# Two interleaved units of a four-layer decoder on one core: own chains, own attention jobs and tables of turns in the second part

## The reference, cut to what matters

```python
# layer 2
x += linear_attention(norm(x)) @ w_proj          # L2a: elu(q)+1, elu(k)+1, causal, 16 heads
x += latent_cross_attention(norm(x), ctx)        # L2x: 16 heads of 64, keys = context and latents
x  = moe_lora_ffn(norm(x))                       # L2f: router, 8 low-rank experts, the best 2
# layer 3
x += delta_rule_mixer(norm(x), conv3, conv15, conv64, gates)  # L3a: triangular inverse per chunk,
                                                 #   three filters, moments, gelu, softmax over 5 paths, rms
x += rotary_cross_attention(norm(x), ctx)        # L3x
x += moe_ffn(norm(x))                            # L3f: 8 experts, the best 2, and a shared one
```

## Time and profile before

| | |
|---|---|
| median of 3 runs | 1779.44 us |
| the profiled execution, its own time | 1794.3 us |
| its span | 1792.9 us |
| mean granted TensorE clock | 0.871 of full |
| part a, first to last matmul | 480.9 us |
| part c, four iterations | 1161.4 us |

### The profile page before, as it was taken

How to read it: one execution, slowest core, us unless ns; L and a number is a source line. 1 busy time by engine, 2 the same in 40 slices (tenths; PEclk the granted TensorE clock), 3 DMA queues, 4 the chain that set the end, 5 groups by cost and what they waited for, 6 DMA issues and landing times. The chain is left out here.

```text
span 1792.9 us, 40153 instructions
## 1 busy us (share of the span) xinstructions
PE 1530.7 (85%) x17496; PEld 1300.6 (73%) x17496; DVE 1100.9 (61%) x2843; ACT 670.3 (37%) x1323; POOL 127.9 (7%) x265
## 2 busy tenths in 40 slices
PE   5888887898886899898879999779989977989986
PEld 3666676776654589797769788668879766978865
DVE  5668678577768566355658445567644565753565
ACT  4343463453547535222315323323422231532331
POOL 2010111111110000100000100000000000010000
PEclk8699998898997889898779988789988777998878
DMA  6000000000000100000000000000000000000000
GB/s 245 1 2 1 1 2 1 1 2 1 2 30 30 61 1 1 1 4 1 1 1 1 1 3 2 1 1 2 1 2 3 1 1 1 1 1 2 3 1 24
DMA packets 6510, 19.87 MB, mean 11 GB/s; under 512 B 2240, under 2 KB 4288, under 8 KB 5824
## 3 DMA queue, kind: packets, MB, share of 16 engines
q1 hardware_dynamic: 6336, 17.32, 2.7%
HBM read 16.27 MB, written 1.05 MB: 10 GB/s over the span
## 5 line engine op out<-in xcount | busy, mean ns | idle before, releaser
L480 PE MATMUL PS<-CC 128*128 128x256 f32 x656 | 197.1, 449 | 20.4 <-DVE mv L457 16.9
L480 PEld LDWEIGHTS PS<-CC 128*128 128x128 f32 x656 | 142.3, 229 | 45.7 <-DVE mv L457 17.7
L1839 PE MATMUL PS<-AR 64*64 64x32 f32 (+1 forms) x3072 | 124.3, 237 | 16.4 <-DVE AR L2112 8.5
L1839 PEld LDWEIGHTS PS<-AR 64*64 64x64 f32 x3072 | 121.5, 156 | 18.1 <-DVE AR L2112 9.0
L469 POOL TENSOR_SCALAR SC<-mv 128x2 f32<-128x2 f32 x96 | 18.6, 194 | 1568.9 <-DVE mv L457 1567.0
L587 PEld LDWEIGHTS PS<-vo,AR 128*64 128x64 f32 x2560 | 111.8, 178 | 25.1 <-issue 15.9
L587 PE MATMUL PS<-vo,AR 128*64 128x18 f32 x2560 | 121.4, 241 | 5.7 <-DVE AR L1493 3.9
L1855 PE MATMUL PS<-AR,PA 64*64 64x204 f32 (+39 forms) x2624 | 123.3, 323 | 2.8 <-issue 2.1
L567 PE MATMUL PS<-CC,AR 128*128 128x128 f32 x512 | 100.7, 343 | 19.9 <-ACT AR L551 19.9
L1855 PEld LDWEIGHTS PS<-AR,PA 64*64 64x64 f32 x2624 | 104.1, 144 | 10.7 <-issue 4.8
L531 DVE TENSOR_REDUCE SC<-PS 128x8 f32<-128x512 f32 x128 | 86.5, 684 | 21.8 <-PE PS L691 21.1
(11 more groups left out here) (405 smaller groups left out, 3114.3 us busy)
## 6 DMA issues: line engine op xcount, KB each, us to landing
WC<-in_cw SPq DMA_DIRECT2D x1, 5438.5 KB, 19.3
PA<-in_fd SPq DMA_DIRECT2D x1, 2624.0 KB, 9.9
PA<-in_stat SPq DMA_DIRECT2D x2, 1280.0 KB, 5.7
out<-X SPq DMA_DIRECT2D x1, 1024.0 KB, 5.1
PA<-in_aw SPq DMA_DIRECT2D x1, 975.0 KB, 10.8
AR<-in_raw SPq DMA_DIRECT2D x1, 832.0 KB, 7.5
CC<-in_const SPq DMA_DIRECT2D x1, 809.0 KB, 7.6
AR<-in_intw SPq DMA_DIRECT2D x1, 576.0 KB, 8.5
```

The costliest lines, as they stand in the source:

```text
L480: T.matmul(st.ps[:, bank, 0:ST], lhsT=ident, rhs=CC[:, 0:ST], start=True, stop=True)
L1839: m = T.matmul(ps[rows, bank, n * width:(n + 1) * width], lhsT=lhs[rows, n, :], rhs=rhs(rows, n), start=True, stop=True)
```

## The change

All of it is in part c. The cross-attention jobs of L2x become a list for each stream with shorter lags, their stages in another order inside a step and with a yield behind each; the shared chains of L3a and L3f become one chain for each stream, with a yield ahead of each wait; the two table loads and the exponential are issued for each stream; and the four tables `AHEAD_C` get uneven numbers. No matmul is added or taken away, nor is a `keep_clock`.

```diff
-        LAG = {"scores": 1, "turn": 4, "weigh": 5, "out": 6}
-        JOBS = [(st, j) for j in range(TS * GR) for st in streams]
+        LAG = {"scores": 1, "turn": 2, "weigh": 3, "out": 3}
+        JOBS = range(TS * GR)
...
-        def tensor_cross():
+        def tensor_cross(st):
             G2, O2 = (cross_w[:, m:m + 2, :, :].rearrange("p m c d -> p (m c) d") for m in (0, 2))
             for n in range(len(JOBS) + LAG["out"]):
-                for st, j in at_lag(n, 0):
+                for st, j in at_lag(st, n, LAG["weigh"]):
+                    d = Cross(st, j)
+                    yield
+                    T.wait_ge(*st.dve.at("L2x.tokens"))
+                    T.wait_ge(*st.act.at(f"{d.name}.turned"))
...
+                    m.then_inc(*st.pe.up(f"{d.name}.weighed"))
+                    yield
+                for st, j in at_lag(st, n, LAG["scores"]):
...
         def tensor_l2_cross(st):
             yield from tensor_norm(st, "L2x")
-            if st.s:
-                tensor_cross()
-            yield
+            yield from tensor_cross(st)
...
-            if st.s:
-                table_for(ACT.Gelu)
+            table_for(ACT.Gelu)
...
-            if st.s:
-                table_for(ACT.Exp)
-            yield
-            if st.s:
-                for u in streams:
-                    A.wait_ge(*u.dve.at(f"{k}.below"))
-                A.activation(SC[:, :, 64:104], SC[:, :, 64:104], ACT.Exp).then_inc(*pair.act.up(f"{k}.exps"))
+            table_for(ACT.Exp)
+            yield
+            A.wait_ge(*st.dve.at(f"{k}.below"))
+            A.activation(sc[:, 64:104], sc[:, 64:104], ACT.Exp).then_inc(*a.up(f"{k}.whole.exps"))
...
-            def both_moments():
-                squares, norms = (SC[:, :, 320:480].rearrange("p s (n m) -> p s n m", m=4)[:, :, :, m] for m in (1, 3))
-                for u in streams:
+            def vector_norm_moments():
+                squares, norms = (SC[:, one, 320:480].rearrange("p s (n m) -> p s n m", m=4)[:, :, :, m] for m in (1, 3))
+                for u in (st,):
+                    yield
                     V.wait_ge(*u.dve.at(f"{k}.moments"))
-                for _ in vector_rsqrt(b, SC[:, :, 112:152], squares, SC[:, :, 152:192]):
-                    pass
+                yield from vector_rsqrt(b, SC[:, one, 112:152], squares, SC[:, one, 152:192])
                 V.wait_ge(*b.now())
...
         AHEAD_C = {
-            "tensor": (1, 2, 3, 4, 5, 6, 7, 8, 9, 10, 11, 12, 13, 14, 15, 16, 17, 18, 19, 20, 21, 22, 23, 24, 25, 26,
...
+            "tensor": (0, 0, 0, 0, 4, 4, 4, 4, 4, 4, 5, 5, 9, 9, 10, 10, 10, 14, 14, 18, 19, 19, 19, 21, 21, 23, 23,
...
```

More of the change, by code:

```diff
@@ L1547, in tensor_cross @@
                     m.then_inc(*st.pe.up(f"{d.name}.queries"))
[L1548 to L1570, removed]
+                    yield
+                if n == 1:
+                    for q in range(SQ):
+                        m = T.transpose(st.ps[:, 3, q * P:(q + 1) * P], st.kvt[:, q, :], ident)
+                    m.then_inc(*st.pe.up("L2x.tokens"))
+                    yield
+                for st, j in at_lag(st, n, LAG["turn"]):
                     d = Cross(st, j)
@@ L1575, in tensor_cross @@
                     m.then_inc(*st.pe.up(f"{d.name}.turned"))
-                for st, j in at_lag(n, LAG["out"]):
+                    yield
+                for st, j in at_lag(st, n, LAG["out"]):
                     d = Cross(st, j)
@@ L1613, in vector_cross @@
                     V.tensor_reduce(d.most, scores, AX, ALU.max).then_inc(*v.up())
+                    yield
                     V.wait_ge(*v.now())
                     V.tensor_tensor(d.blocks, scores, bc(d.most, 2, P), ALU.subtract).then_inc(*v.up(f"{d.name}.below"))
[L1616 to L1628, removed]
+                    yield
+                if n == 1:
+                    V.wait_ge(*st.pe.at("L2x.tokens"))
+                    V.tensor_copy(st.ar[:, 4096:4608], st.ps[:, 3, :]).then_inc(*st.dve.up("L2x.tokens"))
+                    yield
+                for st, j in at_lag(st, n, LAG["out"]):
                     d = Cross(st, j)
@@ L1957, in tensor_l3_attention @@
             yield
-            T.wait_ge(*pair.dve.at(f"{k}.moments", st))
+            T.wait_ge(*v.at(f"{k}.whole.moments"))
             for j in range(TS):
@@ L2155, in both_rms, with vector_path_rms @@
+                V.tensor_tensor(lj, lj, bc(bc(PR5[:, 4:24], 1, TS), 1, 1), ALU.add).then_inc(*b.up(f"{k}.whole.shares"))
+                yield
+            def vector_path_rms():
+                for u in (st,):
+                    yield
                     V.wait_ge(*u.dve.at(f"{k}.mixed_squares"))
-                mx = SC[:, :, 104:112]
+                mx = SC[:, one, 104:112]
                 V.tensor_scalar(mx, mx, 1.0 / 32, 1e-5, ALU.mult, ALU.add).then_inc(*b.up())
-                for _ in vector_rsqrt(b, SC[:, :, 112:120], mx, SC[:, :, 120:128]):
-                    pass
+                yield from vector_rsqrt(b, SC[:, one, 112:120], mx, SC[:, one, 120:128])
@@ L2277, in vector_l3_attention @@
             V.tensor_tensor(lh, logits, bc(mx, 3, 5), ALU.subtract).then_inc(*v.up(f"{k}.below"))
-            if st.s:
-                both_shares()
+            yield from vector_path_shares()
             yield
-            V.wait_ge(*pair.dve.at(f"{k}.shares", st))
+            V.wait_ge(*v.at(f"{k}.whole.shares"))
             for j in range(TS):
```

200 lines of the change are left out of this document (123 added, 77 removed), and 28 rows, old and new, of the table AHEAD_C.

## The result

| | before | after |
|---|---|---|
| median | 1782.7 us (4 runs) | 1681.22 us (4 runs, 1671.38 to 1692.22) |
| ratio, with its 95% interval | | 0.9416 (0.9316 to 0.9516) |
| profiled execution, its own time | 1794.3 us | 1674.83 us |
| its span, mean granted clock | 1792.9 us, 0.871 | 1673.5 us, 0.926 |
| part c | 1161.4 us | 1045.1 us |

What follows compares the result with a forecast made beforehand. TensorE was taken as the bound, losing time to waits and the lower clock. Per iteration 27 gained - 2 chains - 1 loads = 24 us, 96 in four, off the 1779.4 us median: 1684 us forecast, range 1645 to 1725.

Steps and rivals of the forecast that it cites:

- Little comes of it: Rival: both units still wait at the same points, or VectorE limits L3f; 10 us an iteration, 1740 us, chance 0.20.
- L2x as the loser: Rival: L2x loses its seamless matmuls to a late shares or copy and falls to low clock; 1824 us, chance 0.08.
- More: Rival: three quarters of the waits and clock loss go, 42 us an iteration, 1611 us, chance 0.17.
- The waits, 60 us: Part c: half of TensorE's 33.7 us standing per iteration goes, since the other stream's matmuls fill it; 15 us an iteration.
- Of 4.3 I let a third go: L3x: both streams' scores still stand together, so only a third of the 4.3 us wait before them goes.
- The clock, 48 us: Part c: matmul time lost to the lower clock, 24 us an iteration, shrinks by 12 us an iteration.
- If half the waiting goes, I let half of the 24.3 us follow: Part c: clock loss falls in the same share as the waits, giving 12 us an iteration.
- the 33 to 36 expected: Sign in the changed profile: L3x at 33 to 36 us instead of 40.
- The premise under the 24.3: Five stages besides L2x: all standing lies in low stretches, where matmuls cost nearly double; (82.4 - 33.7) / 2 = 24.3 us lost.
- The chains, 8 us: L3a and L3f: separate half-width chains add 7.6 us of VectorE an iteration, 2 of them taken as cost.
- the loads, 4 us: L3a: two activation table loads an iteration become four, 1.283 us each; 1 us an iteration taken as cost.
- The second way: Part c without L2x, given part a's 16.4% share of loss, gains 26 us an iteration, 104 in four.

Runs made afterwards that it cites:

- Experiment 1: Changed kernel with even tables 1, 2, 3, ... in part c, own chains, own jobs and finer steps kept: 1817.72 us, ratio 1.0149.
- experiment 3: Changed kernel with uneven tables only for L3a, L3x and L3f, even ones up to the end of L2f: 1706.94 us, ratio 0.9565.
- experiment 8: Changed kernel with one Newton step instead of three in every vector_rsqrt of part c: 1671.82 us, ratio 0.933.
- experiment 4: Changed kernel with tanh instead of gelu and no table_for in part c, 16 table loads fewer: 1674.19 us, ratio 0.938.
- experiment 12: The changed kernel measured again, unaltered, on another chip: 1679.86 us, ratio 0.9421.
- experiments 7: Changed kernel with twice the keep_clock matmuls in part c: 1753.04 us, ratio 0.9777.
- experiment 10: Changed kernel with seven more keep_clock matmuls at stream 1's step ahead of its scores in L3x: 1713.23 us, ratio 0.9625.
- experiment 9: Kernel before with 8 more keep_clock matmuls in the wait ahead of L3x's scores in stream 0: 1775.26 us, ratio 0.9919.

## Why the prediction was right, and where not

**The time and the mechanism.** Forecast 1684 us, measured 1681.22; 96 us less was forecast, and the medians are 101.5 us apart. The two profiled executions are 119.5 us apart (1794.3 to 1674.83), of them 116.3 in part c: the one before was 11.6 us above its median, the one after 6.4 below. There is one profile of the kernel before, so each term checked on this pair is some us uncertain. Experiment 1 shows that the gain needs the order: the same instructions in even turns are at 1817.7 us. "Little comes of it" (1740) and L2x as the loser (1824) didn't come about: L2x is at 283.6 us against 283.4 in four iterations, with the stages of a job as they were, though 13.4 us of it are now at the lower clock. "More" (1611) is off too.

**The waits, 60 us: too large.** The standing fell by 45.9 us, from 139.8 to 93.9, where "70 to 90" was to be seen. "Of 4.3 I let a third go" in L3x is the step that failed: the wait was split over two scores and its total rose from 17.1 to 19.3 us (all standing in L3x fell by a sixth, 35.5 to 29.3). At the iteration's end (longest wait 1.7 us, "under 3" expected) it was right, and the wait for the experts' second product fell by more than half (11.7 to 4.7).

**The clock, 48 us: too small.** The same matmuls and filler take 70.4 us less, and part c's clock is 0.94, above the 0.90 to 0.93 named. The low time fell by 205 us, from 321 to 116. "If half the waiting goes, I let half of the 24.3 us follow" failed: a third of the standing went and two thirds of the low time. The clock doesn't follow the sum of the waits. L3x shows it, since it came to 31.7 us, under the 33 to 36 expected, with its wait no shorter in sum; so does L3a in experiment 3.

The premise under the 24.3 was wrong too, in two places that partly cancel. It put all standing into low stretches and took a matmul there at double its time (it named up to 41 for the case that no standing lies there). By the clock's records only 25.3 of the 139.8 us of standing in part c lay in low stretches before (9.0 of 93.9 now), and TensorE was busy in them for 295.6 us (107.0 now). That busy time fell by 188.6 us and the matmuls took 70.4 us less, so at the lower level the same matmuls took an estimated 1.6 times their time (188.6 / (188.6 - 70.4)), not twice. The rows agree: 1.05 against 0.65 us for sixteen L587, 1.96 against 1.09 for eight L567 (844.57 in the changed kernel), 4.11 against 2.32 for `keep_clock`, which is 1.6 to 1.8. Each us of low time that went gave back 70.4 / 205 = 0.34 us, in L3x 30.5 / 85.3 = 0.36 (matmul time 128.3 to 97.8).

The Trainium skill ("TensorE: Matmul & The Clock Gate", section "Terms") takes half of the time at the lower level as lost; by that the gain would be an estimated 102 us of matmul time. The measured 70 is less.

The two errors of the sum, 14 us too much for the waits and 22 too little for the clock, partly cancel: that the number came so near is in part luck.

**The chains, 8 us, and the loads, 4 us: nothing.** VectorE has 40.2 us more in part c ("by about 30" expected), with 208 operations more in its windows. A half-width operation alone costs nearly a whole one (L880 takes 227 ns at 40 columns, 300 at 80; the prediction took 194). But the number of operations is not what adds the time: in even turns (experiment 1) the same instructions keep VectorE busy for 641.0 us, 16.8 less than before the change. There the same operation of both streams stands back to back, and their records overlap. L2416 takes 0.24 us for two in experiment 1, and for one in the changed kernel:

```profile
1124.78 0.16 DVE L2416 TENSOR_REDUCE SC<-SC 128x2 f32<-128x16 f32 x1
```

With 22.4 us of such chains taken out (experiment 8) or all 16 loads (experiment 4), part c is not shorter. Both terms belonged at the lower end: this added work of VectorE and ScalarE is off the path. In even turns a chain is exposed: L3f takes 31.7 us more there (experiment 1), 18.6 of it standing (45.2 against 26.6), while its low time rises from 16.7 to 51.2. ScalarE's 8.2 us more were near the 10 expected. The row that the prediction read for "no gap behind" a load shows the idle time ahead of it; the timeline in experiment 4 bears the reading out.

**The second way** to the number (part a's share of loss, 104 us) was nearer to the 116.3 of part c than the sum by terms.

**What stays open:** why a low stretch in L3x ends after 3.4 or 6.8 us in the changed kernel (and in experiment 12 again), and lasts 20 us and more in the kernel before and in experiments 7 and 10. In experiment 9 both lengths occur in one kernel behind the same waits, so the order and the waits just ahead don't decide it alone. With it stays open how much of the clock's 70 us the new order brings for certain and how much by where such stretches happen to end. How much of the gain each engine's table brings, and whether uneven tables would do with the shared chains, wasn't tried either.

## What to carry to other kernels

Where two streams of work share in-order queues, splitting shared chains and ending steps at each wait brought nothing by itself, and cost a little (here 1.5%, 0.6 to 2.4); the order of turns over it brought the gain (here some 7% over the same instructions in even turns). Parts of such tables don't add: the entries of an iteration's start also decide how the end of the iteration before it is filled. When a wait at the head of TensorE's queue is shortened, count the low-clock stretch behind it apart from the wait: here the matmuls' time was the larger part, 70 us of 116. Before placing filler matmuls, read in the order of the queue which stream comes first, and measure: here double filler cost 4%, filler ahead of the wrong one of two waits 2%, and filler in L3x's wait in the kernel before brought 0.8%.

## What the runs showed that was not expected

- The low stretch in L3x is 3.4 us in some places and 20.5 to 27.3 in others, with TensorE busy for 87% of the stage in the longer case (34.95 of 40.2 us, experiment 10). Experiment 9 has both lengths in one kernel, with the same matmuls and waits. A small edit ahead of such a place can cost 30 us: experiment 10 lost 36.8 us of part c for 56 filler records, 30.9 of them in L3x.
- Low time is not half lost: 0.34 to 0.36 us for each us in these stages. Little of a low stretch is standing; these matmuls took 1.6 to 1.8 times as long at the lower level, not twice. Why, the runs don't show.
- The same instructions keep VectorE busy for 641.0 us of part c in even turns and for 697.9 in uneven ones, and the second kernel is the faster by some 7%: the busy time of an engine off the path says little.
- Activation table loads, 1.28 us each, cost nothing measurable at sixteen in part c.
